# A decaying neighbour sum on one core: masks in byte planes, means on the Scalar engine, weight transfers behind x, floors and differences over two beats

## The reference

```python
# x (4096, 64) f32, adj (4096, 4096) of 0.0 and 1.0, about 1 in 256 is 1
h = jnp.maximum(_layernorm(x, axis=-1), 0.0)
support = h @ weight
mask = (adj != 0).astype(support.dtype)
rank = jnp.cumsum(mask, axis=1)
deg = rank[:, -1:]
k = jnp.minimum(deg, 100.0)
pos = rank - (deg - k)
w = mask * jnp.where(pos > 0, 0.5 ** (k - pos), 0.0)
out = x + (w @ support + bias)
```

## Time and profile before

| | us |
|---|---|
| median of 3 runs | 224.29 (223.89 to 224.78) |
| the profiled execution | 224.81 |
| its span | 222.5 |
| PE busy | 202.5 (91%) |
| DVE busy | 203.0 (91%) |
| ACT busy | 161.7 (73%) |
| POOL busy | 28.9 (13%) |
| last tile of adj on the chip | about 168 |

### The profile page before, as it was taken

The page is one execution under the profiler, slowest core; times in us unless marked ns, Lnnn a source line. Parts: engine busy times, 40 slices in busy tenths (PEclk is TensorE's granted clock), DMA queues, the critical chain, the costliest instruction groups (busy, mean ns, idle before and its releaser), DMA issues.

```text
span 222.5 us, 6397 instructions
## 1 busy us (share of the span) xinstructions
PE 202.5 (91%) x2740; PEld 195.6 (88%) x2740; DVE 203.0 (91%) x244; ACT 161.7 (73%) x300; POOL 28.9 (13%) x52
## 2 busy tenths in 40 slices
PE   0367599999999999999999999999999999999994
PEld 0267368999898999999999999999999999999993
DVE  1989989999979999999997999999999998997973
ACT  2331787688687888777787878878887989998710
POOL 8700010221011004002200000300000000000000
PEclk9999769999999999999999999999999999999999
DMA  6999999999999999999999999999980000000001
GB/s 203 186 210 212 214 212 215 215 216 213 215 215 214 216 216 214 215 219 214 218 214 218 215 216 215 218 219 215 218 169 13 3 15 0 15 3 12 15 15 31
DMA packets 8587, 36.12 MB, mean 162 GB/s; under 512 B 1648, under 2 KB 4464, under 8 KB 4464
## 3 DMA queue, kind: packets, MB, share of 16 engines
q0 software_dynamic: 4608, 33.56, 72.7%
q1 hardware_dynamic: 3120, 1.57, 2.9%
q10 hardware_dynamic: 832, 0.59, 0.9%
HBM read 68.22 MB, written 1.05 MB: 311 GB/s over the span
## 4 chain that ended last, share of the span: by engine, by line
PE 84%; DMA 7%; ACT 4%; DVE 3%; POOL 1%; issue 1%; POOLq 0%
PE acc L610 38%; PE chain L603 28%; PE chain L601 16%; DMA adj_b<-in_adj 7%; ACT powers L289 4%; PE chain L589 2%; DVE masks L342 1%; PE acc L572 1%; DVE later L385 1%; DVE part L348 0%; DVE acc L468 0%; POOL adj_b L215 0%; ACT support L263 0%; DVE sum_a L412 0%; DVE sum_b L417 0%
## 5 line engine op out<-in xcount | busy, mean ns | idle before, releaser
L289 ACT ACTIVATE powers<-chain 128x512 int16<-128x512 f32 (+1 forms) x279 | 149.8, 572 | 34.4 <-PE chain L603 34.2
L610 PE MATMUL acc<-support,powers 128*128 128x192 bf16 x1024 | 162.6, 246 | 1.3 <-ACT powers L289 1.1
L603 PE MATMUL chain<-diag_own,masks 128*128 128x128 bf16 x608 | 114.3, 230 | 0.0
L601 PE MATMUL chain<-diag_past,masks 128*128 128x128 bf16 x568 | 109.3, 225 | 3.4 <-ACT powers L289 2.7
L610 PEld LDWEIGHTS acc<-support,powers 128*128 128x128 bf16 x1024 | 99.9, 102 | 3.4 <-issue 2.8
L601 PEld LDWEIGHTS chain<-diag_past,masks 128*128 128x128 fp8e3 x568 | 80.4, 146 | 6.8 <-ACT powers L289 6.8
L603 PEld LDWEIGHTS chain<-diag_own,masks 128*128 128x128 fp8e3 x608 | 85.4, 147 | 0.3 <-issue 0.2
L342 DVE TENSOR_SCALAR masks<-adj_b 128x4096 uint8<-128x4096 bf16 x32 | 72.9, 2281 | 3.5 <-DMA adj_b<-in_adj 3.5
L603 PE MATMUL chain<-diag_step,masks 128*128 128x128 bf16 x416 | 60.1, 221 | 0.0
L603 PEld LDWEIGHTS chain<-diag_step,masks 128*128 128x128 fp8e3 x416 | 54.9, 145 | 0.0
L215 POOL DMA_DIRECT2D adj_b<-in_adj x32 | 24.4, 766 | 111.8 <-DVE masks L342 111.3
(11 more groups left out here) (47 smaller groups left out, 62.7 us busy)
## 6 DMA issues: line engine op xcount, KB each, us to landing
adj_b<-in_adj POOLq DMA_DIRECT2D x32, 1024.0 KB, 34.6
out<-x_sb SPq DMA_DIRECT2D x14, 64.0 KB, 2.2
x_sb<-in_x SPq DMA_DIRECT2D x1, 512.0 KB, 3.9
x_sb<-in_x ACTq DMA_DIRECT2D x1, 512.0 KB, 5.2
out<-x_sb SPq DMA_DIRECT2D x4, 32.0 KB, 9.4
w<-in_L_gnn_weight ACTq DMA_DIRECT2D x2, 16.0 KB, 9.7
bias_b<-in_L_gnn_bias ACTq DMA_DIRECT2D x1, 32.0 KB, 15.1
```

The costliest lines, as they stand in the source:

```text
L289: nc.scalar.activation(powers[:, c, b, cols].bitcast(i16), chain[c][:, cols], ACT.Relu, bias=(MAX_NEIGH + 1) * STEP).then_inc(powers_ready ...
L601: nc.tensor.matmul(chain[c][:, at:at + P], column(n, t + 1), diag_past[:, :], start=False, stop=False, skip_group_check=True)
L603: return nc.tensor.matmul(chain[c][:, at:at + P], column(n, t), diag_own[:, :] if marked else diag_step[:, :], start=False, stop=True, ski ...
L610: return nc.tensor.matmul(acc[u % ACCS][:, k * 3 * D:(k + 1) * 3 * D], powers[:, u % FLIGHT, s + 1 if k < MARKS[u] else s, at:at + P], sup ...
```

## The change

- The mask's bytes are laid out in planes. With r runs of a tile (256, or 512 in the units of four runs), the byte pair of columns 2j and 2j+1 of run r stands in plane j beside the same pair of all other runs. DVE now reads adj in pairs of bf16 that lie one run apart (32 bytes, or 16) and writes in order. `column` then reads its 128 bytes 4 bytes apart (8 in the units of four runs). The three halvings add planes: all their operands are in order.
- `BATCH` is 2: twice the floors and differences, each half as long.
- The means and the variance's scaling go from DVE to ACT. ACT squares both halves ahead of the first two relus, and takes the root ahead of the third.
- The weights' two transfers go from ACT's queue to SP's, behind x's first half. The bias stays on ACT's queue.
- DVE's opening order is new: both sums of squares before the first mask, the deviation, the third halving and the scan of unit 0 before mask 1; two scales before the third halving of unit 1, and the scan of unit 1 behind mask 2. PE turns block 2 before the first product with the weights. In the slots, parts and take-offs move by one slot.
- The bias is added in two instructions, not four. Mask and first two halvings of a unit come one slot later in program order. Lags: five shrink by 2 or 3, nine by 1, three stay, unit 2's grows by 2. Unit 8 starts one slot earlier.

```diff
-    BATCH = 4
+    BATCH = 2
-    STARTS = [0, 5, 6, 14, 23, 27, 34, 40, 46, 51, 57, 63, 68, 74, 80, 85, 91, 97]
-    LAGS = [7, 5, 8, 11, 11, 10, 11, 10, 10, 11, 11, 12, 12, 12, 11, 11, 10, 9]
+    STARTS = [0, 5, 6, 14, 23, 27, 34, 40, 45, 51, 57, 63, 68, 74, 80, 85, 91, 97]
+    LAGS = [7, 4, 10, 9, 9, 9, 10, 8, 9, 9, 8, 12, 11, 11, 11, 10, 9, 8]
+        RUNS_OF = [CHAINS[UNIT_OF[n]] * P for n in range(NT)]
+        def planes_of(n):
+            return masks[:, (n + SHIFT) % RING, :].rearrange("q (j r e) -> q j r e", r=RUNS_OF[n], e=2)
+        def in_planes(tensor, n):
+            return tensor.rearrange("q (r j e) -> q j r e", r=RUNS_OF[n], e=2)
...
+            sp.wait_ge(w2_zeroed, 2)
+            sp.dma_start(w2[0:D, 0:D], weight).then_inc(weight_loaded, 16)
+            sp.dma_start(w2[D:2 * D, D:2 * D], weight).then_inc(weight_loaded, 16)
...
-            act.wait_ge(w2_zeroed, 2)
-            act.dma_start(w2[0:D, 0:D], weight).then_inc(weight_loaded, 16)
-            act.dma_start(w2[D:2 * D, D:2 * D], weight).then_inc(weight_loaded, 16)
...
+            def means(f):
+                act.wait_ge(sum_ready, f + 1)
+                nc.scalar.activation(per_row(mean, f), per_row(row_sum, f), ACT.Copy, scale=1.0 / D).then_inc(mean_ready, 1)
             def root():
-                act.wait_ge(ln_step, 1)
+                act.wait_ge(sq_sum_ready, 2)
+                nc.scalar.activation(var_eps[:, :], sq_sum[:, :], ACT.Copy, scale=1.0 / D, bias=EPS).then_inc(var_ready, 1)
+                act.wait_ge(var_ready, 1)
...
+            means(0)
+            means(1)
             square(0)
+            square(1)
             turn_h(0)
             turn_h(1)
-            square(1)
+            root()
             turn_h(2)
             turn_h(3)
-            root()
...
-                nc.vector.tensor_scalar(masks[:, (n + SHIFT) % RING, :], adj_b[:, n % LOADS, :], 0.0, 1.0,
+                nc.vector.tensor_scalar(planes_of(n), in_planes(adj_b[:, n % LOADS, :], n), 0.0, 1.0,
                                         ALU.not_equal, ALU.mult).then_inc(mask_ready, 1)
...
+            def halve(u, ins, outs, done):
+                h = outs.shape[2]
+                return nc.vector.tensor_tensor(outs, ins[:, :, 0:h], ins[:, :, h:2 * h], ALU.add).then_inc(done, 1)
...
             row_sums(0)
-            means(0)
             row_sums(1)
             center(0)
-            means(1)
             center(1)
             sq_sums(0)
+            sq_sums(1)
             mask(0)
-            sq_sums(1)
             halve_1(0)
-            variance()
+            deviation()
             halve_3(0)
+            scan(0, 0)
+            mask(1)
             halve_2(0)
-            mask(1)
-            scan(0, 0)
             halve_1(1)
-            deviation()
+            scale(0)
             halve_2(1)
             scale(1)
+            scale(2)
             halve_3(1)
-            scale(0)
-            scan(1, 0)
-            scale(2)
             scale(3)
             mask(2)
+            scan(1, 0)
...
-                    if u >= 3 and to == 9 and FIRST[u] > 3:
+                    if u >= 3 and to == 8 and FIRST[u] > 3:
                         mask(FIRST[u])
...
-                    if u >= 3 and to == 7:
+                    if u >= 3 and to == 6:
                         halve_1(u)
-                    if u >= 3 and to == 6:
+                    if u >= 3 and to == 5:
                         halve_2(u)
...
             def column(n, t):
-                return masks[:, (n + SHIFT) % RING, :].bitcast(fp8).rearrange("q (p t) -> q p t", t=T)[:, :, t]
+                h = CHAINS[UNIT_OF[n]]
+                run, col = t // (T // h), t % (T // h)
+                return planes_of(n).bitcast(fp8).rearrange("q j (p h) e -> q j p h e", h=h)[:, col // 2, :, run, col % 2]
...
             turn_h(1)
+            turn_h(2)
             make_support(0)
-            turn_h(2)
+            turn_h(3)
             make_support(1)
-            turn_h(3)
```

More of the change, by code:

```diff
@@ L145, in gnn_decay_kernel @@
         ln_step = sem("ln_step")
+        var_ready = sem("var_ready")
+        rough_ready = sem("rough_ready")
+        rstd_ready = sem("rstd_ready")
         std_ready = sem("std_ready")
@@ L271, in signs @@
                     act.wait_ge(chain_ready[u % FLIGHT], taken_until(u) + TAKEN[u])
-                at = slice(j * N // PIECES, (j + 1) * N // PIECES)
-                nc.scalar.activation(masks[:, (n + SHIFT) % RING, at].bitcast(i8), adj_b[:, n % LOADS, at],
+                runs = slice(j * RUNS_OF[n] // PIECES, (j + 1) * RUNS_OF[n] // PIECES)
+                nc.scalar.activation(planes_of(n).bitcast(i8)[:, :, runs, :], in_planes(adj_b[:, n % LOADS, :], n)[:, :, runs, :],
                                      ACT.Sign).then_inc(signs_ready, 1)
@@ L311, in _ @@
                 if g == 2:
+                    part(1, 0)
                     part(2, 0)
@@ L341, in mask, with words @@
                     dve.wait_ge(chain_ready[u % FLIGHT], taken_until(u) + TAKEN[u])
-                nc.vector.tensor_scalar(masks[:, (n + SHIFT) % RING, :], adj_b[:, n % LOADS, :], 0.0, 1.0,
+                nc.vector.tensor_scalar(planes_of(n), in_planes(adj_b[:, n % LOADS, :], n), 0.0, 1.0,
                                         ALU.not_equal, ALU.mult).then_inc(mask_ready, 1)
[L345 to L349, removed]
+            def halve(u, ins, outs, done):
+                h = outs.shape[2]
+                return nc.vector.tensor_tensor(outs, ins[:, :, 0:h], ins[:, :, h:2 * h], ALU.add).then_inc(done, 1)
+            def words(room, u, planes):
+                k, w = SIZES[u], planes * CHAINS[u] * P
+                return room[:, 0:k * w].rearrange("q (k w) -> q k w", k=k)
             def halve_1(u):
@@ L354, in halve_1 @@
                 dve.wait_ge(mask_ready, n + k)
-                halve(u, masks[:, at:at + k, :].rearrange("q k n -> q (k n)").bitcast(u16),
-                      part1[:, 0:k * N // 4].rearrange("q (c t) -> q c t", t=STEPS[u] // 4), STEPS[u] // 4, halved)
+                halve(u, masks[:, at:at + k, :].bitcast(u16), words(part1, u, STEPS[u] // 4), halved)
             def halve_2(u):
@@ L361, in halve_2 @@
                     return
-                k = SIZES[u]
                 dve.wait_ge(halved, halved_until(u) + 1)
-                halve(u, part1[:, 0:k * N // 4], part2[:, 0:k * N // 8].rearrange("q (c t) -> q c t", t=STEPS[u] // 8),
-                      STEPS[u] // 8, halved)
+                halve(u, words(part1, u, 4), words(part2, u, 2), halved)
             def halve_3(u):
-                k, h = SIZES[u], CHAINS[u]
                 dve.wait_ge(halved, halved_until(u + 1))
@@ L373, in halve_3 @@
                     dve.wait_ge(later_ready, FIRST[u - SUMS + 1])
[L374 to L377, removed]
+                halve(u, words(part2 if CHAINS[u] == 2 else part1, u, 2),
+                      runs_of(sums, sums_4, u)[:, :, 0:CHAINS[u] * P], sums_ready)
             def scan(u, k):
@@ L427, in row_sums @@
                 nc.vector.reduce_sum(per_row(row_sum, f), half_of(x_sb, f), AX.X).then_inc(sum_ready, 1)
[L429 to L432, removed]
             def center(f):
@@ L473, in add_bias @@
                 dve.wait_ge(bias_loaded, 16)
-                rows = slice(f * T // 4, (f + 1) * T // 4)
+                rows = slice(0, T // 4) if f == 0 else slice(T // 4, T)
+                n = rows.stop - rows.start
                 nc.vector.tensor_tensor(x_sb[:, rows, :], x_sb[:, rows, :],
-                                        bias_b[:, :].unsqueeze(1).to_broadcast([P, T // 4, D]),
+                                        bias_b[:, :].unsqueeze(1).to_broadcast([P, n, D]),
                                         ALU.add).then_inc(xb_ready, 1)
             row_sums(0)
-            means(0)
             row_sums(1)
             center(0)
-            means(1)
             center(1)
             sq_sums(0)
+            sq_sums(1)
             mask(0)
-            sq_sums(1)
             halve_1(0)
-            variance()
+            deviation()
             halve_3(0)
+            scan(0, 0)
+            mask(1)
             halve_2(0)
-            mask(1)
-            scan(0, 0)
             halve_1(1)
-            deviation()
+            scale(0)
             halve_2(1)
             scale(1)
+            scale(2)
             halve_3(1)
-            scale(0)
-            scan(1, 0)
-            scale(2)
             scale(3)
             mask(2)
+            scan(1, 0)
             halve_1(2)
```

40 lines of the change are left out of this document (15 added, 25 removed).

## The result

The changed kernel takes 219.3 us (219.15 to 219.51), the kernel before 224.45 in the same comparison: 0.9776 of it, 95% interval 0.9751 to 0.980. The forecast was 218.5 in a range of 215.5 to 223.8. The total is right, and so is the mechanism that carries the pace. But the terms behind it are not all right: the largest one but one, the start, brought next to nothing in this kernel, and something else stood in its place, so that the sum came out right in part by luck.

A forecast was written before the change was run, and what follows sets the result against it. PE was taken as the bound for the last 140 us, DVE 3% behind. From 224.8: -2.8 start, -3.0 pace, -0.5 lags, +0.5 DVE beside PE gives 219.0, 218.5 by the median; range 215.5 to 223.8.

The forecast's parts named there:

- the start: Before 80 us: DVE's new opening order brings an early lead between 2.3 and 3.4 us; 2.8 us taken.
- The bound: PE sets the pace for the last 140 us, with DVE only 3% behind it.
- The pace: PE after 80 us: faster count loads bring a triple from 203 to 194 ns; 3.0 us taken, bounds 0 and 3.2.
- DVE: Mask stays at 2.28 us, third halving falls to 0.42; DVE's balance over the kernel about -1.2 us, at most +3.
- 0 either way: At the start: the weights' transfers should land some 2 us earlier behind x's first half, worth 0 us.
- the floor of 68.4: Earliest start of unit 6: tile 10 lands at 62.53, its mask, halvings and two scans take about 5.8 us.
- The lags: Shorter lags move products of two units in flight to before 80 us: 1.3 us at most, 0.5 taken.
- The mask's later slot: Mask one slot later in program order costs 0: tiles of that stretch land later than they are asked for.
- The price of small batches: On DVE: 52 extra floors and differences cost about 75 ns each, 3.9 us, with 8.1 us as upper bound.
- The dtype: Rival: count loads are slow because they are fp8, staying at 146 ns with pace 203; 221.5 us; chance 0.17.
- The mask's price: Rival: DVE's mask pays for reading pairs; no gain from about 2.6 us a mask, near 285 at 4.4; chance 0.11.
- DVE becomes the end: Rival: added instructions overlap less, DVE gains 3 us, pace gain lost; 224 to 225 without the lead; chance 0.10.

The follow-up runs named there:

- the pitch alone: Kernel before, only the count's weight load changed to read wrong mask bytes 4 bytes apart instead of 32 (output not the reference's): 219.64 us, 0.9812.
- singles: Changed kernel, mask reading one bf16 each 32 bytes instead of a pair (output not the reference's), one run: 268.3 us.

## Why the prediction was right, point by point

**The bound.** Right: PE's pace after 80 us, with DVE just behind. The pitch alone moved the time by 4.2 us, with nothing of DVE's changed.

**The pace.** Right in mechanism and per matmul (203 to 195 ns, loads of 146 to 99). The 3.0 us for the 358 pairs after 80 us were nearly right too: between the bases of units 7 and 17 the pitch alone brought 2.55 us, and PE waited 0.7 us there. Too small was what I gave to the pairs before 80 us, 1 us, under the start: the pitch alone brought 2.3 us ahead of unit 7, and 4.2 us in all.

**DVE.** Mask, halving, floor and difference are right within 10 ns; the 17 shorter halvings of the working are 16. That the 0.27 us of a halving is worth nothing by itself was not: the planes alone are 1.3 us faster than the pitch alone, and PE waits less for scans.

**The start: the step that failed.** "0 either way" for the weights' transfers was wrong. I looked at who waits for them, not at whom they push aside: their move, and with it the earlier bias, held the first tile up by about 2 us, and unit 6's base came 0.7 us earlier instead of 2.8. The order on DVE behaved as worked out; with the transfers back it gave 12.07, 20.67 and a base of unit 7 1.6 us earlier. Even then the term was too large, for the faster loads take most of the same room. With the planes alone, and the old opening, unit 6's base stands here:

```profile
69.13 0.39 PE L598 MATMUL chain<-diag_base,later 128*128 128x128 bf16 x4
```

That is 2.7 us earlier than in the earlier trace rows, in an execution whose granted clock was 0.95 over the first 35 us, against 0.90 before, and only 0.7 us above the floor of 68.4. What stood in the start's place in the sum was thus the early pace and DVE's shorter halving: the planes alone bring 2.4%, some 5.5 us, nearly the whole 5.8. That this made up for the missing start is luck.

**The lags.** Taken as 0.5 by themselves; the runs show no gain alone (0.9792 beside 0.9756), and 0.6% for opening and lags together. The mask's later slot, put at 0, belongs to that 0.6%, as far as the traces show: with unit 8's earlier start it puts the scans ahead of the mask.

**The price of small batches.** The instructions cost what was said. That the balance of DVE left it as full as PE was said too, and priced at 0.5 us; with a lead to keep, the small batches cost 0.7%, 1.1 us by the medians (218.45 against 217.34).

**The rivals.** The dtype is out; its 221.5 had also kept the 1 us that faster loads give to the start, so it was 0.5 to 1 us too low. The mask's price was real for singles and zero for pairs: at 3.9 us a mask the kernel took 268 us, where the rival had 285 for 4.4. "DVE becomes the end" came half true: DVE is full from 80 to 200 us and has no gap left to give, but PE is never idle there.

## What to carry to other kernels

When matmuls of 128 columns alternate with fresh weights, read the starts of successive matmuls against columns divided by clock; a surplus behind two loads in a row points to the load, and the pitch of its bytes is the first thing to look at: 8 (one run) or less was fast enough here, 16 was not. When a small transfer is moved to another queue, ask first what it will delay, and look at the landing of the first big tile. Here an early lead was worth something only when no later engine was full and when the work that the next unit waits for stood ahead of other work in DVE's order; so measure such edits together, not only one by one.

## What was not expected of the hardware

A load of 128 fp8 weights took 99, 113, 145 and 146 ns at pitches of 4, 8, 16 and 32 bytes. DVE read one bf16 every 32 bytes in 3908 ns for 4096 elements, but a pair every 32 bytes in 2281, as fast as in order. Moving two transfers of 16 KB from one hardware queue to another, and a third of 32 KB forward by it, went with a landing of the first megabyte of a third queue at 12.7 to 13.9 us instead of 11.6 to 12.1.
